# Attention with all heads written out, without work past the last head, and the feed-forward part begun in the last head

## The reference

```python
x = _layernorm(x + mamba(x))          # L0 mixer: state-space scan, 512 channels, 16 states
x = _layernorm(x + experts(x))        # L0 feed-forward: router, 4 experts, the best 2 weighted
x = _layernorm(x + attention(x))      # L1 mixer
x = _layernorm(x + ffn(x))            # L1 feed-forward

def attention(x):                     # B=2, T=2048, 16 heads of 16
    q, k, v = split(x @ Wq.T + bq), split(x @ Wk.T + bk), split(x @ Wv.T + bv)
    q_stp, k3, v3 = q @ Wqs.T + bqs, k @ Wks.T + bks, v @ Wvs.T + bvs
    cross_kv = jnp.cross(k3, v3, axis=-1)
    scores = (q @ k^T + q_stp @ cross_kv^T) * temp
    out = softmax(scores) @ v
    return merge(out) @ Wo.T + bo

def ffn(h):
    return relu(h @ W1 + b1) @ W2 + b2
```

## Time and profile before

| | us |
|---|---|
| median of 3 runs | 3821.85 |
| lowest and highest | 3819.26, 3822.27 |
| profiled execution | 3819.2 |
| its span, first to last instruction | 3817.4 |
| first score product of the attention part, from the span's start | 1998.1 |
| first transposes of the feed-forward part | 3517.8 |
| first up product of the feed-forward part | 3538.4 |
| TensorE busy in the span | 3385.6 (89%) |
| VectorE busy | 2945.8 (77%) |
| ScalarE busy | 2222.2 (58%) |
| GpSimd busy | 1508.8 (40%) |

### The profile page before, as it was taken

The page is one execution under the profiler, slowest core; times in us unless marked ns, Lnnn a source line. Parts: engine busy times, 40 slices in busy tenths (PEclk is TensorE's granted clock), DMA queues, the critical chain, the costliest instruction groups (busy, mean ns, idle before and its releaser), DMA issues. The chain is left out here.

```text
span 3817.4 us, 50051 instructions
## 1 busy us (share of the span) xinstructions
PE 3385.6 (89%) x14561; PEld 1587.7 (42%) x14561; DVE 2945.8 (77%) x3571; ACT 2222.2 (58%) x3640; POOL 1508.8 (40%) x1294
## 2 busy tenths in 40 slices
PE   4339899898888989899979999999999999999998
PEld 1115555454554546455533232323232323233666
DVE  5898797978879787985438888888788888887343
ACT  5345565656556565553127777777677777776221
POOL 3988787887878788885010000000000000000110
PEclk8669999999999999999989999999999999999999
DMA  2111122122222212223111000000000000001010
GB/s 104 32 38 61 56 71 91 61 87 72 72 65 75 85 61 83 70 80 127 56 46 50 18 18 18 18 18 18 19 18 18 18 18 18 18 18 35 22 33 28
DMA packets 111209, 183.03 MB, mean 48 GB/s; under 512 B 14623, under 2 KB 84663, under 8 KB 102393
## 3 DMA queue, kind: packets, MB, share of 16 engines
q1 hardware_dynamic: 110969, 180.13, 14.9%
HBM read 153.99 MB, written 26.09 MB: 47 GB/s over the span
## 5 line engine op out<-in xcount | busy, mean ns | idle before, releaser
L1894 DVE TENSOR_REDUCE tile_max<-ps 128x1 f32<-128x1024 f32 x1028 | 1210.9, 1220 | 253.3 <-PE ps L1685 250.5
L1835 ACT ACTIVATE probs<-ps 128x512 f32<-128x512 f32 x2056 | 1115.9, 598 | 374.4 <-PE ps L1699 348.7
L1437 POOL TENSOR_TENSOR vals<-vals,c_sb 128x512 f32<-128x512 f32 x512 | 673.0, 1346 | 275.9 <-DVE state L1244 275.8
L1238 DVE TENSOR_TENSOR_SCAN vals<-stacks,state,ps 128x512 f32<-128x512 f32 x512 | 655.0, 1279 | 99.2 <-POOL heads_v L1448 28.1
L1699 PE MATMUL ps<-stacks 101*128 101x512 bf16 x2056 | 708.1, 382 | 13.6 <-ACTq L1842 12.4
L1448 POOL TENSOR_TENSOR heads_v<-heads_v,vals 128x512 f32<-128x512 f32 x512 | 638.9, 1280 | 8.7 <-issue 0.2
L1685 PE MATMUL ps<-stacks 99*128 99x512 bf16 x2056 | 614.4, 379 | 0.0
L1709 PE MATMUL ps<-probs,heads_v 128*32 128x512 f32 x4096 | 547.7, 605 | 5.5 <-issue 5.5
L231 POOL COPY heads_v<-vals 128x256 f32 (+1 forms) x32 | 12.6, 401 | 1345.1 <-PE ps L1709 1322.0
L746 PE MATMUL ps<-e_w,hid 128*128 128x256 f32 x2048 | 472.2, 389 | 38.4 <-issue 33.4
L722 PE MATMUL ps<-x1T,e_w 128*128 128x512 f32 x1024 | 467.5, 601 | 35.4 <-ACT hid L1005 35.4
(11 more groups left out here) (181 smaller groups left out, 2941.0 us busy)
## 6 DMA issues: line engine op xcount, KB each, us to landing
e_w<-in_e_w SPq DMA_DIRECT2D x64, 1024.0 KB, 7.0
c_sb<-scratch_c SPq DMA_DIRECT2D x128, 256.0 KB, 3.4
stacks<-scratch_q SPq DMA_DIRECT2D x210, 64.0 KB
stacks<-scratch_k SPq DMA_DIRECT2D x210, 64.0 KB
scratch_q<-parts SPq DMA_DIRECT2D x16, 384.0 KB, 4.3
scratch_k<-parts SPq DMA_DIRECT2D x16, 384.0 KB, 4.2
xr<-scratch_x SPq DMA_DIRECT2D x10, 512.0 KB, 4.2
xn_tok<-in_x SPq DMA_DIRECT2D x8, 512.0 KB, 4.9
```

Of the source, the lines that this page charges most:

```text
L1238: v.tensor_tensor_scan(h[:, n % 2, m, :], decay[:, n % 2, m, :], ps[:, 0, :], state[:, n, m:m + 1], ALU.mult, ALU.add).then_inc(s["h_ready ...
L1437: last = nc.gpsimd.tensor_tensor(h[:, n % 2, m, :], h[:, n % 2, m, :], c_sb[:, n % C_RING, :], ALU.mult)
L1835: fn(probs[:, step % 2, qc, :], ps[:, S_BANK[i], :], ACT.Exp)\
L1894: v.tensor_reduce(tile_max[:, t, half:half + 1], ps[:, slot(side):slot(side) + PAIR, :].rearrange("p a n -> p (a n)"), AX.X, ALU.max).then ...
```

## The change

It does four things, all in `attention_ffn`. The loops over heads become straight code for 32 heads on all five engines, with constants in place of registers. Maxima of heads past the last, the turning of head 32's maxima, steps 0 and 1 of head 32 and the loads for heads past the last are left out (`if u >= heads: return` and the like); slots of the maximum banks are now counted by a running number instead of by formula, with the same alternation. Chunk 0's stages move into head 31: `turn_o` behind step 4's values, `copy_o` behind step 5's exponentials, `project_o` behind step 8's values, `turn_x3` behind step 13's, `copy_x3` behind step 14's exponentials; VectorE's `stage_o`, `norm3` and the next `stage_o` stand between head 30's `normalise` and head 31's. Since `turn_values` of head 31 may use bank 5, it waits for `copy_x3`. And SyncE issues the first two loads of x2 ahead of the heads' loads.

The core of the diff:

```diff
@@ SyncE
-            with sp.Fori(0, heads // ROT) as r:
-                for j in range(ROT):
-                    u = r * ROT + j
-                    load_neg(sp, sh, scr, s["passed_sp"], u + 1, (j + 1) % ROT)
+            load_x2(0, 0)
+            load_x2(1, 1)
+            for u in range(heads):
+                if u + 1 < heads:
+                    load_neg(sp, sh, scr, s["passed_sp"], u + 1, (u + 1) % ROT)
+                if u + 3 < heads:
                     wait_alone(sp, s["passed_sp"], s["scores_mm"], u * PER_HEAD + 1)
-                    load_stack(sp, sh, scr, (u + 3) & (HEADS - 1), (j + 3) % ROT)
+                    load_stack(sp, sh, scr, u + 3, (u + 3) % ROT)
@@ TensorE
-            with pe.Fori(0, batches) as b:
-                for quad in range(quads):
-                    four_heads(b * quads + quad)
...
-            pe.wait_ge(s["weights"], 96)
-            pe.wait_ge(s["probs_ready"], heads * PER_HEAD + 2 * STEP + CREDIT)
-            pe.wait_ge(s["max_read"], M_BASE + heads * M_PER_HEAD + FOLD_USE + 1)
-            turn_o(0)
-            project_o(0)
-            turn_x3(0)
+            step_of(0, 0)
+            step_of(0, 1)
+            for u in range(heads):
+                values(u, 0)
+                for step in range(2, KT):
+                    step_of(u, step)
+                    if step == TURN_STEP and u + 1 < heads:
+                        turn_max(u + 1)
+                    values(u, step - 1)
+                    if u == heads - 1 and step == 4:
+                        pe.wait_ge(s["weights"], 96)
+                        turn_o(0)
+                    if u == heads - 1 and step == 8:
+                        project_o(0)
+                    if u == heads - 1 and step == 13:
+                        turn_x3(0)
+                step_of(u + 1, 0)
+                values(u, KT - 1)
+                step_of(u + 1, 1)
+                if u == heads - 1:
+                    pe.wait_ge(s["x3T_ready"], 1)
+                turn_values(u)
+            pe.wait_ge(s["probs_ready"], heads * PER_HEAD)
+            pe.wait_ge(s["max_read"], turn[0])
             with pe.Fori(0, chunks - 1) as c:
@@ ScalarE
-            copy_o(0)
-            copy_x3(0)
+            exps(0, 0)
+            exps(0, 1)
+            for u in range(heads):
+                for step in range(2, KT):
+                    exps(u, step)
+                    if u == heads - 1 and step == 5:
+                        act.wait_ge(s["weights"], 96)
+                        copy_o(0)
+                    if u == heads - 1 and step == 14:
+                        copy_x3(0)
+                exps(u + 1, 0)
+                copy_values(u)
+                exps(u + 1, 1)
@@ VectorE
-            stage_o(0, 0)
-            norm3(0)
-            stage_o(1, 1)
...
+                step_of(u + 1, 0)
+                step_of(u + 1, 1)
+                if u == heads - 1:
+                    stage_o(0, 0)
+                    norm3(0)
+                    stage_o(1, 1)
+                normalise(u)
```

More of the change, by code:

```diff
@@ L1731, in step_of @@
+            def step_of(u, step):
+                if u >= heads:
+                    return
                 if step == 0:
[L1732 to L1741, removed]
@@ L1761, in _ @@
-            with pe.Fori(0, batches) as b:
-                for quad in range(quads):
-                    four_heads(b * quads + quad)
+                    pe.wait_ge(neg_loaded[u % ROT], 16 * (u // ROT + 1))
+                scores(u, step, 0)
+                next_max(u, step, 0)
+                scores(u, step, 1)
+                scores(u, step, 2)
+                next_max(u, step, 1)
+                scores(u, step, 3)
             def turn_o(c):
@@ L1840, in copy_values @@
                 fn(av[:], ps[:, AV_BANK, :], ACT.Copy).then_inc(s["av_copied"], 1)
-            act.sem_inc(s["probs_ready"], CREDIT)
-            exps(0, 0)
-            exps(0, 1)
-            def four_heads(r):
-                for j in range(ROT):
-                    u = r * ROT + j
-                    for step in range(2, KT):
-                        exps(u, step)
-                    exps(u + 1, 0)
-                    copy_values(u)
-                    exps(u + 1, 1)
-            with act.Fori(0, batches) as b:
-                for quad in range(quads):
-                    four_heads(b * quads + quad)
-            act.wait_ge(s["weights"], 96)
             def copy_o(c):
@@ L1962, in norm4 @@
                            ysum[:], ln_tmp, s["passed_dve"])
-            stage_o(0, 0)
-            norm3(0)
-            stage_o(1, 1)
+            step_of(0, 0)
+            step_of(0, 1)
+            for u in range(heads):
+                for step in range(2, KT):
+                    step_of(u, step)
+                    if u + 1 < heads:
+                        if step == TURN_STEP - 1:
+                            row_maxima(nc, dve, sh, turn[0])
+                        if step == TURN_STEP:
+                            use = turn[0]
+                            negate(nc, dve, sh, ps[0:KT, next_slot(), 0:P], use, u + 1)
+                step_of(u + 1, 0)
[5 more added lines that the diff above has]
+                normalise(u)
             with dve.Fori(0, chunks - 1) as c:
@@ L1978, in stage @@
                 stage_values(nc, sh, j, b, hd)
[L1980 to L1988 removed]
+            for u in range(ROT, heads):
+                b, hd = divmod(u, NH)
+                if hd == 0:
+                    pool.wait_ge(s["v_loaded"], 16 * (b + 1))
+                stage(u, b, hd, u % ROT)
             pool.wait_ge(s["weights"], 96)
```

162 lines of the change are left out of this document (54 added, 108 removed).

## The result

The changed kernel took 3793.66 us (median of 4 runs, 3792.14 to 3794.54), the kernel before 3822.06 in the runs beside it (4 runs, 3819.26 to 3822.87). The ratio is 0.9927, 95% interval 0.9909 to 0.9944: faster by 28.4 us, where 36.9 were forecast. The time lies in the range of the prediction and 8.7 us above its number.

What follows compares the result with a forecast made beforehand. TensorE was taken to set the pace, a ring the steps without maxima. 8.9 + 10.7 - 7.5 + 22.6 + 2.2 = 36.9 us off 3819.2 gave 3782.3, plus 2.65 for the median: 3785.0; range 3775 to 3797.

Steps and rivals of the forecast that it cites:

- batch boundary: End of head 15: two pauses at the taken branch of the loop over batches go in straight code; saves 8.9 us.
- steps without maxima: 24 steps from step 8 of head 30: value product, exponential, score product ring sets 2.37 us against 2.83; saves 10.7.
- inserted work: Chunk 0's transposes, projection and ScalarE copies put into the last head lengthen its ring; costs 7.5 us, bounds 0 and 7.5.
- passage: From head 31's last step to chunk 1's transposes: 28.98 us before, 6.4 after; saves 22.6 us (21 to 23).
- clock: TensorE keeps its full clock, narrowly, at the start of the feed-forward part; saves 2.2 us (0 to 2.2).
- a step other than 2.83 in heads 1 to 29: Sign of being wrong: steps in heads 1 to 29 no longer take 2.83 us.
- a rival at 5%: Register instructions ahead of the loops' waits were on TensorE's path; removing them saves 46 us more, 3739 us; 5%.
- the rival by which the straight code is not there in time: Straight code reaches TensorE late; a 5.5 us pause in each of 32 heads, 176 us, gives 3961 us; 3%.
- the one by which the pause stays: The batch boundary's pause was no branch and stays; 3794 us; 10%.
- ScalarE was to be busy for nine tenths of a step: Sign of being right: ScalarE busy nine tenths, value products 2.37 us apart, from step 9 of head 30 on.
- The forecast's case, with 65%: All terms hold as summed, 36.9 us saved, likeliest time 3785 us; 65%.
- its 3789 to 3794: Rival: the clock falls one to three times inside the last head and the passage loses its 2.2 us; 15%.

Runs made afterwards that it cites:

- waits_all: Changed kernel with the order of two waits swapped on TensorE, VectorE and ScalarE, late wait written first; 3782.54 us, ratio 0.9891.
- passage_back: Changed kernel with chunk 0's feed-forward stages put behind the last head again, heads written out and maxima left out as before; 3805.75 us, ratio 0.9961.
- waits_pe: Changed kernel with only the order of the two waits swapped on TensorE, at the turnings of maxima and values; 3785.41 us, ratio 0.9901.
- fourth_bank: The kernel with score banks in turn over all heads, plus a fourth score bank in head 31 from its step 4 on; 3749.04 us, ratio 0.9806.
- turn_later: The kernel with waits swapped on all three engines, plus each turning moved behind one more call of value products on TensorE; 3764.78 us, ratio 0.9844.
- banks_in_turn: The kernel with the turnings moved later, plus the scores' PSUM banks taken in turn over all heads, not restarted each head; 3755.92 us, ratio 0.9824.

## Why the prediction was right or wrong, point by point

| term | forecast, us | measured, us | from |
|---|---|---|---|
| batch boundary | 8.9 | 8.9 | 1435.36 less waits_all's 1426.51 |
| heads 0 to 30 otherwise | 0 | -8.2 | after's 1434.68 less 1426.51 |
| steps without maxima | 10.7 | 9.8 | 70.39 less passage_back's 60.61 |
| inserted work | -7.5 | -6.5 | 67.14 less 60.61 |
| passage | 22.6 | 22.9 | 27.36 less 4.51 |
| clock | 2.2 | 2.2 | 280.95 less 278.75 |
| sum | 36.9 | 29.1 | the time from the first values moved by 28.98 |

**The heads.** This is the step that failed. The prediction let heads 1 to 29 stand at 2.83 us a step and had no term for them; it named "a step other than 2.83 in heads 1 to 29" as what would prove it wrong. The plain steps are that still (2.84); three places of each head, which were longer before too, have grown. I had asked of the register instructions only whether their removal would free TensorE (a rival at 5%), and not what they did to the waits around them: they had kept the late wait on the transposes. The order of the program shows both waits of a turning in one bracket, and I did not ask which of the two the instruction carries. 0.275 us a head, unrounded, times 30 heads is 8.2 us, all that is missing. waits_pe and waits_all give them back one by one, and waits_all's 3782.54 lies 2.5 us below the forecast of 3785.

**The boundary.** Right: no pause is left, and the group of value products has no idle time before it, where the earlier trace rows had 5.5 us. The trace before records TensorE's branch itself, a compare and branch from 2754.56 to 2758.32 us, in the first of the two pauses. For the second, 1.94 us, no record names what TensorE waits for; shown is only that it went with the branch. By the Trainium skill ("Runtime: NRT & Kernel Launch", section "Instruction fetch mechanics") the fetching of straight code is mostly hidden; the trace agrees, with 32 heads written out and no pause on TensorE at any of their ends but the 0.33 us for VectorE. The rival by which the straight code is not there in time is refuted, and so is the one by which the pause stays.

**The steps without maxima.** Right in mechanism, shown by fourth_bank. The size of a step was 2.37, in waits_all it is 2.40, and the 0.06 up to 2.46 is the same matter of waits, on ScalarE. Over 20 plain steps 2.46 for 2.37 is 1.8 us; the odd steps, which I had priced singly, came out some 0.9 better together. The 0.32 us from the last score product to the values are there as forecast. One sign of being right failed: ScalarE was to be busy for nine tenths of a step, and it is for 2.07 us of 2.46 (3450.91 to 3453.37), 84%, since the 2.23 us were not its work alone. The rule of the Trainium skill on weight loads pulled ahead ("TensorE: Matmul & The Clock Gate", section "Step-by-step: what each phase is for") would have given 0.09 us a step more; the trace, with 0.32 us, shows none of it between these two kinds of product.

**The inserted work.** The transposes and the projection cost TensorE about what they take, as spacings over the plain 2.46: 0.92 for each of the transposes (1.1 forecast), 3.55 for the projection and 0.29 in the step behind it (3.45 forecast). The copies were too dear in my sum: each cost 0.42 us and not 0.9, since the score products are done while ScalarE copies, and its exponentials run back to back behind the copy:

```profile
3478.41 1.05 ACT L1822 ACTIVATE oT<-ps 128x1024 f32<-128x1024 f32 x1
3479.32 2.11 ACT L1813 ACTIVATE probs<-ps 128x512 f32<-128x512 f32 x4
3481.82 2.06 ACT L1813 ACTIVATE probs<-ps 128x512 f32<-128x512 f32 x4 [0.39 <-PE ps L1683]
```

VectorE's sum and normalisation were covered, as forecast: they start at 3490.00 us and end at 3497.20, the transposes of x3 are at 3502.36, and the step's pause there is that of every step.

**The passage and the clock.** Right in size, 6.02 us for 6.4, and the 22.9 us are 3.4 of scores and maxima left out (27.36 less passage_back's 23.95) and 19.4 of stages moved. "Kept, narrowly" was literally so, below.

**The chances.** The forecast's case, with 65%, is what happened, but for the term that no case had. That the time lies in the range is luck in part. It was the range's upper part, made for other rivals, that took it in: the clock did not fall in the last head, which is what its 3789 to 3794 stood for.

## What to carry to other kernels

Where an instruction waits for two semaphores, write the one that comes last first, so that it sits on the instruction and not ahead of it, and look at that order again whenever register instructions near it come or go: here it was worth 0.28 us a head, over a fifth of the gain that the change could have had (8.2 of 28.98 and 8.2). Better still, ask of each short wait that recurs whether the waiting instruction can stand one call later: 0.23 us in front of two small turnings looked like nothing, and moving the turnings gave 21 us from the first values on, 17.8 in the medians. And where a step is set by a ring through a buffer, count what each engine takes back to back, without the gaps in the row, before naming the bound that a further buffer would uncover.

## What the hardware did that I had not expected

A lone wait has a price. From the start of VectorE's reduction to TensorE's transposes were 1.28 us where the late wait sits on the transposes (3325.87 to 3327.15, as in the earlier trace rows), and 1.37 where it stands ahead of them (2760.45 to 2761.82). On VectorE it was 0.07 us (3.41 to 3.35 at the turning of the maxima, before rounding 3.414 to 3.346) and on ScalarE 0.06 (2.46 to 2.40), by the two runs on waits.

The clock at the passage hangs on little. The changed kernel and waits_all have nearly the same two short pauses there, ahead of the turning of the values and ahead of the transposes of chunk 1: 0.76 and 1.19 us in the former, 0.81 and 1.19 in the latter. The changed kernel kept its full clock; waits_all, whose steps ahead of it are 0.06 us shorter, fell to the half level, 1.2 of 2.4 GHz, a microsecond of either, the changed kernel's first, in the view by stretches (PE, PEld, DVE, ACT, POOL; granted clock; DMA), and the chain of waits_all:

```profile
3513.00:3514.00 1.00, 1.00 (x9) 0.76 (x8) 0.00 (x0) 0.26 (x1) 0.00 (x0) 1.00 0.00 0
3502.00:3503.00 1.00, 1.00 (x7) 1.00 (x6) 0.00 (x0) 0.00 (x0) 0.00 (x0) 0.50 0.00 0
```

```profile
3501.54 1.96 PE ps L1730 x8
3503.51 14.48 PE ps L1756 x32
```

Its feed-forward part took 280.37 us from chunk 1's transposes on, the changed kernel's 278.75: 1.6 us more. turn_later and banks_in_turn fell too (280.43 each), waits_pe and fourth_bank didn't (278.74 and 278.75). The length of the two pauses doesn't part them: it is 0.81 and 1.19 us in all of these four. Each is one profile, so what decides it stays open; by the rows, a gain or a loss of 1.6 us there has nothing to do with what the edits were for.
